# The second half of the tokens normalised by ScalarE instead of GpSimd, in both norms of a two-norm transformer block

## What is computed

```python
h = _layernorm(x, axis=-1) * (1 + ca) + sa
x = x + ga * _L0_attn_ref(h, ...)          # softmax(window_softmax(q k / 4)) v, then Wo
h = _layernorm(x, axis=-1) * (1 + cb) + sb
x = x + gb * _L0_ffn_ref(h, W_fc, W_proj)  # square(relu(h W_fc)) W_proj, spikes counted
...
def _layernorm(x, axis=-1, eps=1e-05):
    m = jnp.mean(x, axis=axis, keepdims=True)
    v = jnp.var(x, axis=axis, keepdims=True)
    return (x - m) / jnp.sqrt(v + eps)
```

## Time and profile before

| | us |
|---|---|
| Time, median of 3 runs | 2334.8 |
| the three runs | 2334.80, 2330.03, 2336.23 |
| Time of the profiled execution | 2336.34 |
| its span, first to last instruction | 2334.5 |
| TensorE busy | 2192.1 (94% of the span) |
| VectorE busy | 1732.6 (74%) |
| ScalarE busy | 1510.2 (65%) |
| GpSimd busy | 1166.3 (50%) |

### The profile page before, as it was taken

One profiled execution on the slowest core, in us unless ns is written; L12 is line 12 of the kernel. 1 busy time (PEld: TensorE's weight loads), 2 busy tenths in 40 slices (PEclk: granted clock), 3 DMA queues, 4 the chain that ended last, 5 costly groups with the idle time before them and its releaser, 6 DMA issues.

```text
span 2334.5 us, 47167 instructions
## 1 busy us (share of the span) xinstructions
PE 2192.1 (94%) x19388; PEld 1241.9 (53%) x19388; DVE 1732.6 (74%) x2115; ACT 1510.2 (65%) x2101; POOL 1166.3 (50%) x1126
## 2 busy tenths in 40 slices
PE   6889889999999999999999999999999999989998
PEld 4444344465555555455554555545555555545567
DVE  6787888767787676876778776776877767787466
ACT  2477676766666667676776666766666666667741
POOL 3144134545665456744676257763576544443540
PEclk8999999999999999999999999999999999999999
DMA  5233122211122113111133202231022211101000
GB/s 181 72 107 98 49 55 82 85 48 39 50 68 85 53 35 91 60 51 53 35 91 96 59 9 59 67 109 49 14 65 78 84 35 46 40 16 31 6 28 25
DMA packets 114067, 140.26 MB, mean 60 GB/s; under 512 B 8648, under 2 KB 86760, under 8 KB 113856
## 3 DMA queue, kind: packets, MB, share of 16 engines
q1 hardware_dynamic: 113856, 137.24, 20.7%
HBM read 74.28 MB, written 58.74 MB: 57 GB/s over the span
## 4 chain that ended last, share of the span: by engine, by line
PE 77%; DVE 15%; ACT 3%; DMA 2%; issue 2%; POOL 2%; SPq 1%; ACTq 0%; POOLq 0%
PE pv L822 11%; PE sums L812 9%; PE ring L772 9%; PE score L742 9%; PE score L797 9%; PE sums L754 9%; DVE e L1178 6%; PE score L691 5%; DVE negmax L1156 4%; PE ring L851 4%; PE score L706 3%; PE ring L775 2%; PE score L800 2%; PE score L682 2%; ACT e L1052 2%
## 5 line engine op out<-in xcount | busy, mean ns | idle before, releaser
L1052 ACT ACTIVATE e<-score 128x512 f32<-128x512 f32 x1152 | 670.9, 595 | 400.7 <-PE score L800 220.6
L1178 DVE TENSOR_TENSOR e<-ring,e 128x1024 f32<-128x1024 f32 x576 | 677.5, 1217 | 282.6 <-PE ring L851 281.9
L1156 DVE TENSOR_REDUCE negmax<-ring 128x8 f32<-128x1024 f32 x576 | 679.5, 1220 | 140.5 <-PE ring L775 133.9
L1057 ACT ACTIVATE e<-e 128x2048 f32<-128x2048 f32 x288 | 548.6, 1905 | 3.7 <-DVE e L1178 3.6
L797 PE MATMUL score<-q_st,k_st 112*128 112x512 bf16 (+3 forms) x1536 | 459.7, 331 | 39.2 <-ACT e L1052 22.0
L772 PE MATMUL ring<-k_st,q_st 96*128 96x512 bf16 (+3 forms) x1664 | 389.1, 319 | 53.7 <-DVE e L1178 25.1
L1493 POOL TENSOR_SCALAR r_p<-r_b,ab 128x256 bf16<-128x256 f32 x96 | 88.6, 923 | 531.8 <-DVE r_b L1184 531.8
L822 PE MATMUL pv<-e,v 128*17 128x512 f32 (+3 forms) x3072 | 314.1, 496 | 1.1 <-DVE o_t L1196 1.1
L812 PE MATMUL sums<-e,d_ones 128*32 128x256 f32 x4608 | 304.6, 382 | 1.3
L1472 POOL TENSOR_TENSOR gT<-gT 128x512 f32<-128x512 f32 x112 | 115.9, 1040 | 333.5 <-ACT gT L1025 333.5
L797 PEld LDWEIGHTS score<-q_st,k_st 112*128 112x128 bf16 x1536 | 147.8, 97 | 228.9 <-issue 118.6
(11 more groups left out here) (149 smaller groups left out, 2518.3 us busy)
## 6 DMA issues: line engine op xcount, KB each, us to landing
q_st<-q_parts SPq DMA_DIRECT2D x31, 768.0 KB, 5.9
k_st<-k_parts SPq DMA_DIRECT2D x31, 768.0 KB, 8.6
q_parts<-qk_p SPq DMA_DIRECT2D x30, 384.0 KB, 2.6
k_parts<-qk_p SPq DMA_DIRECT2D x28, 384.0 KB, 2.5
x_in<-in_x SPq DMA_DIRECT2D x8, 1024.0 KB, 5.6
q_parts<-qk_p SPq DMA_DIRECT2D x30, 256.0 KB, 2.9
x_res<-in_x SPq DMA_DIRECT2D x30, 256.0 KB, 4.4
k_parts<-qk_p SPq DMA_DIRECT2D x28, 256.0 KB, 2.9
```

The source lines that it names most:

```text
L1052: act.activation(e[:, n % ES, hh, :], score[SCORE_SLOT["st", n, hh][0]][:, :], ACT.Exp, scale=DK ** -0.5).then_inc(e1_done, 1)
L1057: act.activation(v, v, ACT.Exp).then_inc(e2_done, 1)
L1156: dve.tensor_reduce(negmax[:, at:at + NB // heads, hh:hh + heads].rearrange("p w h -> p h w"), slot[:, :].rearrange("p (h a n) -> p h a n" ...
L1178: dve.tensor_tensor(v, ring[no % 2][:, :].rearrange("p (i n) -> p i n", i=2), v, ALU.mult).then_inc(ring_free, 1)
```

## The change

GpSimd's `normalise` and its 14 calls of four tiles are taken out. VectorE gets one more small instruction behind each `newton` of these norms: `shift` writes -mean * rstd of tiles 4 to 7 into `ln_b`. ScalarE gets a `normalise` that computes rstd * x + shift with its Identity function, with two operands that hold one value for each partition (bias and scale). It does two tiles at the end of one step and two at the end of the next: for the second norm at the ends of steps s = 18 and 19, for the first norm at the end of steps s = 35 and s = 0, and for batch 1's first norm at the ends of steps 7 and 8 of the program. Each pair first waits for `shift`.

```diff
+            def normalise(no, k, src, rstd, shifted, done):
+
+                act.wait_ge(shifted, no)
+                for i in range(NB // 2 + 2 * k, NB // 2 + 2 * k + 2):
+                    act.activation(x_in[:, i, :], src[:, i, :], ACT.Identity, bias=ln_b[:, i:i + 1], scale=rstd[:, i:i + 1]).then_inc(done, 1)
...
+                for k in range(2):
+                    if s == max(LN2_AT) + 3 + k and 0 < b < B:
+                        normalise(b, k, x_res, rstd2, shift2, xn2[1])
+                    if (n + 1 - k) % PERIOD == 0 and 1 < (n + 1 - k) // PERIOD + 1 < B:
+                        normalise((n + 1 - k) // PERIOD + 1, k, x_in, rstd1, shift1, xn1[1])
+                    if n == 7 + k:
+                        normalise(1, k, x_in, rstd1, shift1, xn1[1])
...
+            def shift(no, own, done_no, mv, rstd, shifted):
+
+                dve.wait_ge(own, done_no)
+                at = slice(NB // 2, NB)
+                dve.scalar_tensor_tensor(out=ln_b[:, at], in0=mv[:, at, 0], scalar=-1.0, in1=rstd[:, at], op0=ALU.mult, op1=ALU.mult).then_inc(shifted, 1)
...
                     newton(r, aggr1, exp1_done, newton1, mv1, ln_b, rstd1)
+                    shift(r, newton1, 4 * r + 4, mv1, rstd1, shift1)
                     normalise(r, range(4), x_in, mv1, rstd1, newton1, xn1[0])
...
-            def normalise(r, tiles, src, mv, rstd, own, done):
-                pool.wait_ge(own, 4 * r + 4)
-                for i in tiles:
-                    pool.tensor_scalar(x_in[:, i, :], src[:, i, :], mv[:, i, 0:1], rstd[:, i:i + 1], ALU.subtract, ALU.mult).then_inc(done, 1)
...
-                    if q == max(LN2_AT) + 2:
-                        normalise(r, range(4, NB), x_res, mv2, rstd2, newton2, xn2[1])
...
-                for r, k in ([(b + 2, s - 35)] if b + 2 < B else []) + ([(1, n - 7)] if b == 0 else []):
-                    if k == 0:
-                        normalise(r, range(4, NB), x_in, mv1, rstd1, newton1, xn1[1])
```

More of the change, by code:

```diff
@@ L483, in build @@
         xn1 = [sem("xn1_first"), sem("xn1_second")]
+        shift1, shift2 = sem("shift1"), sem("shift2")
         xn2 = [sem("xn2_first"), sem("xn2_second")]
@@ L1408, in step @@
                         newton(r, aggr2, exp2_done, newton2, mv2, ln_b, rstd2)
+                        shift(r + 1, newton2, 4 * r + 4, mv2, rstd2, shift2)
                         normalise(r, range(4), x_res, mv2, rstd2, newton2, xn2[0])
```

## The result

Over 22 executions of each kernel, the median went from 2332.43 us (2327.76 to 2338.56) to 2338.02 us (2333.85 to 2342.51). The ratio is 1.0024, with a 95% interval of 1.0016 to 1.0031: 5.6 us slower, 3.7 to 7.2. The forecast was +5.7 us. Its absolute figure, 2340.5, lies 2.5 us higher than the result, because it started from the median of three executions (2334.8), and 22 give 2332.4.

A forecast was written before the change was run, and what follows sets the result against it. TensorE, busy 94% of the span and 77% of the chain, was taken as the bound. Terms 2.8 + 1.0 + 1.85 + 0 = 5.65, say 5.7 us, on 2334.8 gave 2340.5 us; 8-in-10 range 2334.0 to 2346.5.

The forecast's parts named there:

- The pairs: On ScalarE, 28 pairs: each instruction takes 596 ns, each pair delays what follows by 0.97 us, bounds 0.6 to 1.5.
- Rival A: Every pair on ScalarE holds it for 1.5 us: 12.6 us slower in all, 2347.4 us; chance 0.12.
- The turns into batches 2 to 6: End of step 0, five turns: an exponential comes 0.37 us late and TensorE waits, 1.85 us in all, bounds 0 to 4.5.
- batch 2's steps 35 and 36: Batch 2's first norm: step 36's first exponential 0.4 us late, step 0's pair adds 0.6; together 1.0 us.
- Rival B: Delays are absorbed; only batch 1's wait shows, shortened by the clock: 1.1 to 2.8 us, 2336.8 us; chance 0.18.
- Batch 1: First norm, steps 7 and 8: ScalarE waits for `shift`, delaying the maxima and `k_st`; 2.8 us, bounds 1.1 to 3.8.
- it is all on the last chain, so 2.8 us pass through: Batch 1, steps 7 and 8: the delay through `m_sb`, the DMAs and `k_st` costs its full 2.8 us.
- at most 1.7 us back: Behind batch 1's load of `k_st`: TensorE's lower-clock stretch may shorten or vanish, returning up to 1.7 us; left open.
- The second norms: Seven norms, steps 18 and 19: pairs cost 0, with 0.1 us to spare at step 18; 2.8 in all if pairs take 1.5.
- the first tile there waits for the end of a GpSimd instruction anyway: VectorE, five second norms beside a split: `shift`, 0.2 us with its gap, is hidden and costs 0.
- Rival C, port relief: Second norms: GpSimd's `normalise` holds VectorE through the port lock; removing it gives 4 us faster, 2330.7 us; chance 0.08.
- The sum: Whole kernel: 2.8 + 1.0 + 1.85 + 0 = 5.65, say 5.7 us slower; 2340.5 us, +0.24%; chance 0.62.

The follow-up runs named there:

- e3: The change for the first norms of batches 2 to 7 only, other norms left on GpSimd; +4.7 us against the kernel before (1.6 to 7.5).
- e7: The change with batch 1's pairs a step later and tile 7 of the turns' first norms moved into step 1; +4.7 us against the kernel before.
- e4: The change for batch 1's first norm only, all other norms left on GpSimd; +1.4 us against the kernel before (-1.2 to 4.0).
- e8: The change with batch 1's pairs at the ends of steps 8 and 9 instead of 7 and 8; +4.7 us against the kernel before.
- e1: The change, but batch 1's first norm stays on GpSimd; +4.2 us against the kernel before (1.4 to 7.2).
- e5: The kernel before, with GpSimd's second-half tiles of the middle norms cut to one column of 256; ratio 1.0003 against the kernel before.
- e9: The kernel before, with GpSimd's split of QK held until VectorE's four second-norm tiles are done; -10.0 us against the kernel before.
- after: The kernel with the whole change, against the kernel before it; median 2338.02 us, ratio 1.0024.
- e2: The change for the seven second norms only, all first norms left on GpSimd; +1.9 us against the kernel before (-0.9 to 4.4).

## Why the prediction was right, and where it was wrong

- *The pairs.* Right: 591 ns for 596, and the next instruction starts 0.98 to 1.00 us later for 0.97. Rival A (1.5 us) falls.
- *The turns into batches 2 to 6 and batch 2's steps 35 and 36.* Right in place and size: 1.81 for 1.85, 0.88 for 1.0, and e3 (3.0 ± 0.4) and e7 (2.2 ± 0.5 back) bear it out over many executions. Rival B, that such delays are absorbed, falls for these. One wait of 0.4 us was absorbed, at a DMA in batch 2.
- *Batch 1.* The mis-sized term: 2.8 us forecast, 1.0 to 1.4 found in like traces (0.6 over all of them). The times say 0.3 to 1.5 ± 0.4 (e4) and 0.3 to 1.5 ± 0.5 (e8); e1 says 1.4 to 2.6 ± 0.5 and alone would not exclude 2.8. The wait of ScalarE, the late `m_sb` and the late `k_st` all came as written, the last two at 3.2 us. The failed step is "it is all on the last chain, so 2.8 us pass through". The chain there also held a stretch at the lower clock behind the load, and the loads' 2.38 us of idle time. The text named the first as open ("at most 1.7 us back") and then left it out of the value taken; in every trace with the wait it went, and the idle time shrank (it did so in e7 and e8 too); 2.9 us were given back together. The term's lower bound, 1.1, was about the right value.
- *The second norms.* 0 forecast, about +0.6 in the trace: 6 x 0.125 - 0.14. The pair is free, as said. `shift` isn't: "the first tile there waits for the end of a GpSimd instruction anyway" was wrong: `shift` itself ends only with GpSimd's cast (0.53 us), and the first tile then runs beside the next GpSimd instruction. The text also counted five such norms beside a split; there are six. The last gives back about as much as `shift` takes, as said.
- *Rival C, port relief.* Falls by e5, and by the tiles at 4.05 us. But its idea was right for another instruction, and worth 10 us (e9).
- *The sum.* By the traces: 1.2 (batch 1) + 0.9 + 1.8 + 0.6 - 0.1 for absorbed waits = 4.4 us. Of after's mean clock, lower by 0.0012, about 0.0007 is batch 1's longer stretch, whose price is in the 1.2 already. The other 0.0005 is worth 0.8 us at 1.65 us per 0.001. Together that is 5.2 of the 5.6 measured (3.7 to 7.2), with an error of some tenths on each part. So it was partly luck that the forecast's sum met the result: a term too large by 1.4 to 1.8 stood in for 0.6 at the second norms and for about 0.8 of clock, which the sum didn't hold. That the change makes the clock fall more often elsewhere is not shown. Of the variants, e2, e3 and e7 also ran 0.0009 to 0.0019 below the kernel before on their chip, e1, e4 and e8 0.0006 to 0.0008, e5 not at all; each has an error of 0.0005. That stays open.

## What to carry to other kernels

Price an instruction that is put on a queue by its hold minus the gap behind it, place by place: that came out within 0.12 us at each of the six turns between batches. Before passing a delay through a wait in full, look at what stands behind that wait, because an idle stretch and a stretch at the lower clock can move with it and pay much of it back. Before correcting times for the clock, look where the clock is low: a stretch that delays nothing must not be credited. And when an engine is slow beside another, compare start times for each instruction of the other: the relief is in holding back the one that overlaps (two lines, 10 us), not in moving the one that comes later.

## What the runs showed of the hardware that I had not expected

- A small VectorE instruction with two SBUF inputs (128x4) took 0.16 us alone, 0.53 us beside a GpSimd cast, ending within 0.01 us of it, and 1.01 us beside a GpSimd TENSOR_TENSOR at the turns between batches, ending within 0.02 us of that.
- VectorE's TENSOR_SCALAR on 128x256 took 0.35 us alone (four in 1.38), 0.40 beside GpSimd's TENSOR_SCALAR of the same shape, and 1.2 to 1.3 beside GpSimd's TENSOR_TENSOR: two kinds of GpSimd work that look alike cost VectorE 15% or a factor of three.
- TensorE's clock falls to 0.50 for a few us at places that differ from execution to execution. With 1.65 us for 0.001 of mean clock, this explains most of the spread of these times, and bringing times to equal clock narrowed the error of a comparison of 12 executions to 0.4 us.
